# Last attention of a four-layer transformer on one core: reciprocal sums through device memory, and a row maximum in two parts

## The reference, cut to what matters

```
q = (LN(x) Wq) / 8                      # 1024 x 64
k = [LN(x) ; LN(ctx)] Wk                # 1101 rows: 1024 tokens and 77 of context
s = q k^T (+ mask on the 77)            # 1024 x 1101
p = exp(s - rowmax(s));  o = (p v) / rowsum(p)
x = x + gate * (LN(concat of heads o Wout) * g + b)
```

## Time and profile before

| | |
|---|---|
| Median of three runs | 2100.9 us |
| Profiled execution, its time | 2084.4 us |
| Profiled execution, its span | 2082.6 us |
| Busy: TensorE, VectorE, ScalarE, GpSimd | 1921.5, 1435.7, 978.5, 752.3 us |
| Mean granted TensorE clock over the span | 0.963 |
| Stage 6 | about 1096 to 1996 us of the span |

### The profile page before, as it was taken

How to read it: one execution, slowest core, us unless ns; L and a number is a source line. 1 busy time by engine, 2 the same in 40 slices (tenths; PEclk the granted TensorE clock), 3 DMA queues, 4 the chain that set the end, 5 groups by cost and what they waited for, 6 DMA issues and landing times.

```text
span 2082.6 us, 33216 instructions
## 1 busy us (share of the span) xinstructions
PE 1921.5 (92%) x11797; PEld 1355.2 (65%) x11797; DVE 1435.7 (69%) x2676; ACT 978.5 (47%) x2079; POOL 752.3 (36%) x1145
## 2 busy tenths in 40 slices
PE   6997799696999988997878999999999999998999
PEld 3885799542699976883565666666675666655644
DVE  5775111467344457787867999999878999998755
ACT  5672333343111252226875555555545555555455
POOL 1002111000522200000006777777656777777500
PEclk9897899898999999998989999999999999999999
DMA  3702899502489960002002333333222333333201
GB/s 115 208 2 79 273 323 333 170 1 86 163 292 321 310 228 1 1 1 86 1 13 60 82 83 82 83 83 83 72 57 72 82 82 82 82 82 81 63 1 41
DMA packets 191184, 226.87 MB, mean 109 GB/s; under 512 B 28939, under 2 KB 167085, under 8 KB 191021
## 3 DMA queue, kind: packets, MB, share of 16 engines
q1 hardware_dynamic: 183725, 201.98, 33.0%
q0 software_dynamic: 7296, 22.78, 3.3%
HBM read 127.64 MB, written 29.91 MB: 76 GB/s over the span
## 4 chain that ended last, share of the span: by engine, by line
PE 45%; ACT 6%; DVE 3%; issue 1%; POOL 0%; ACTq 0%; DVEq 0%; POOLq 0%
PE ps L640 41%; ACT w_odd L1796 4%; PE ps L1214 2%; PE ps L1215 1%; ACT arena L1785 1%; PE ps L1106 0%; DVE w_odd L2532 0%; DVE small L2410 0%; POOL arena L1908 0%; ACT out_feat L1708 0%; PE ps L1115 0%; ACT xn_tok L1651 0%; DVE small L2522 0%; ACT out_feat L1714 0%; DVE arena L2380 0%
## 5 line engine op out<-in xcount | busy, mean ns | idle before, releaser
L1908 POOL COPY arena<-w_odd 32x512 f32<-32x512 f32 x1024 | 623.7, 609 | 254.4 <-DVE w_odd L2532 202.1
L640 PE MATMUL ps<-arena,w_odd 128*128 128x128 f32 (+4 forms) x2352 | 468.2, 441 | 3.0 <-DVE arena L2202 1.2
L640 PE MATMUL ps<-arena 128*64 128x256 f32 (+4 forms) x3248 | 392.3, 370 | 8.3 <-DVE arena L2333 4.4
L640 PEld LDWEIGHTS ps<-arena 128*64 128x64 f32 (+4 forms) x3248 | 258.9, 155 | 119.5 <-issue 22.6
L2532 DVE STREAM_TRANSPOSE w_odd<-w_odd 128x1024 f32<-128x1024 f32 x256 | 317.4, 1245 | 14.6 <-ACT w_odd L1796 3.0
L1796 ACT ACTIVATE w_odd<-ps,small 128x1101 f32<-128x1101 f32 x256 | 301.6, 1179 | 48.0 <-DVE small L2522 41.0
L640 PEld LDWEIGHTS ps<-arena,w_odd 128*128 128x128 f32 (+3 forms) x2352 | 286.3, 188 | 27.9 <-issue 18.7
L1781 ACT ACTIVATE arena<-ps 77x256 f32<-77x256 f32 x128 | 48.5, 379 | 295.4 <-PE ps L1215 295.4
L2522 DVE TENSOR_REDUCE small<-ps 128x1 f32<-128x1101 f32 x128 | 166.9, 1304 | 29.3 <-PE ps L640 28.1
L1893 POOL DMA_INDIRECT token_rows<-arena x62 | 59.8, 964 | 292.3 <-DVE arena L2223 292.3
L2523 DVE TENSOR_REDUCE small<-ps 128x1 f32<-128x1024 f32 x128 | 155.4, 1214 | 0.0
(11 more groups left out here) (398 smaller groups left out, 2909.8 us busy)
## 6 DMA issues: line engine op xcount, KB each, us to landing
arena<-w_odd SPq DMA_DIRECT2D x1024, 64.0 KB
w_odd<-in_s_w SPq DMA_DIRECT2D x32, 1024.0 KB, 7.4
w_odd<-in_s_wgu SPq DMA_DIRECT2D x30, 704.0 KB, 6.1
w_even<-in_s_w SPq DMA_DIRECT2D x15, 1024.0 KB, 7.3
arena<-expert_rows_in SPq DMA_DIRECT2D x62, 130.0 KB, 4.7
w_odd<-in_s_wd SPq DMA_DIRECT2D x30, 256.0 KB, 3.6
out_feat<-in_s_wgu SPq DMA_DIRECT2D x10, 704.0 KB, 5.9
expert_rows_in<-zero_row POOLq DMA_DIRECT2D x1, 5070.0 KB, 33.2
```

Of the source, the lines that this page charges most:

```text
L640: return pe.matmul(o, lhsT, rhs, start=start, stop=stop, **kw)
L1908: pool.tensor_copy(s6_d[u % 4][32 * j:32 * j + 32, :, 256 * i:256 * i + 256], s6_pm[u % 2][32 * i:32 * i + 32, :, 256 * j:256 * j + 256]). ...
```

## The change

The diff has two parts. First, the reciprocals no longer become rows on TensorE. On even u, ScalarE issues a transfer of the four reciprocal columns of a group (128 partitions x 4 words) to a small array in device memory, written word by word; on the following odd u it waits for that transfer and issues two that read the rows back, each row broadcast over 64 partitions. `sums_turn`, its bank and ScalarE's copy L1785 go. VectorE's product waits for the transfers instead. Second, head 0's maximum is taken over bank 0 (512 columns) after the third count of a6_s, over the other 589 columns after the fourth, and the two are joined along two words.

```diff
+        rows_dram = nc.dram_tensor("sum_rows", [2, 2, 2, P], F32).ap()
...
-            if even and 2 <= u < NU + 2:
-                batch += [("r", (u - 2) // 2)]
...
-                def sums_turn(g):
-
-                    pe.wait_ge(a6_rb, g + 1)
-                    bank = free_bank(("r", g))
-                    for i in range(2):
-                        for h in range(2):
-                            r = 64 * h
-                            last = mm(PS[r:r + 64, bank, i * P:(i + 1) * P], s6_rc[:, g % 2, 2 * i + h:2 * i + h + 1].broadcast_to([P, DH]), ident[:, :])
-                    last.then_inc(r6_mm, 1)
...
-                    if even and 2 <= u < NU + 2:
-                        sums_turn((u - 2) // 2)
...
+                    if even and 2 <= u < NU + 2:
+                        g = (u - 2) // 2
+                        act.wait_ge(a6_rb, g + 1)
+                        if g >= 2:
+                            act.wait_ge(rows_in, 32 * (g - 1))
+                        act.dma_start(rows_dram[g % 2].rearrange("i h q -> q (i h)"), s6_rc[:, g % 2], allow_slow_non_contiguous=True).then_inc(rows_out, 16)
+                    if not even and 3 <= u < NU + 3:
+                        g = (u - 3) // 2
+                        act.wait_ge(rows_out, 16 * (g + 1))
+                        if g >= 2:
+                            copied(act, ("v", g - 2))
+                        for h in range(2):
+                            act.dma_start(s6_r[g % 2][64 * h:64 * h + 64].rearrange("p (i q) -> p i q", i=2),
+                                          rows_dram[g % 2][:, h].partition_broadcast(64)).then_inc(rows_in, 16)
...
-                    if even and 2 <= u < NU + 2:
-                        g = (u - 2) // 2
-                        bank = filled(("r", g))
-                        act.activation(s6_r[g % 2], PS[:, bank, 0:2 * P], ACT.Copy).then_inc(r6_act, 1)
...
-                        copied(dve, ("r", g))
+                        dve.wait_ge(rows_in, 32 * (g + 1))
                         dve.tensor_tensor(s6_ot[c][:, q0:q0 + 2 * P], PS[:, bank, 0:2 * P], s6_r[g % 2], ALU.mult).then_inc(r6_dve, 1)
...
+                        dve.tensor_reduce(s6_hm[:, u % 2, 0:1], psf[:, 0:512], AX.X, ALU.max, negate=True)
                         dve.wait_ge(a6_s, 4 * u + 4)
-                        dve.tensor_reduce(s6_nm[:, u % 2, 0:1], s6_sc[0], AX.X, ALU.max, negate=True).then_inc(a6_mx, 1)
+                        link(dve.tensor_reduce(s6_hm[:, u % 2, 1:2], psf[:, 512:KV], AX.X, ALU.max, negate=True))
+                        dve.tensor_reduce(s6_nm[:, u % 2, 0:1], s6_hm[:, u % 2], AX.X, ALU.min).then_inc(a6_mx, 1)
...
-                                dve.wait_ge(r6_mm, r6_no["r", g - 2] + 1)
+                                dve.wait_ge(rows_out, 16 * (g - 1))
```

More of the change, by code:

```diff
@@ L230, in build @@
         s6_gb = cut(small, 400, 4, KD)
-        s6_cm, s6_nm = cut(small, 420, 2, 2), cut(small, 424, 2, 2)
+        s6_cm, s6_nm, s6_hm = cut(small, 420, 2, 2), cut(small, 424, 2, 2), cut(small, 444, 2, 2)
         s6_sm, s6_rc = cut(small, 428, 2, 4), cut(small, 436, 2, 4)
@@ L307, in build @@
         r6_mm, r6_act, r6_dve = sem("r6_mm"), sem("r6_act"), sem("r6_dve")
+        rows_out, rows_in = sem("rows_out"), sem("rows_in")
         t6_done, copied6, t6_base = t5_c, t5_f, NT
@@ L394, in build @@
             for key in batch:
-                eng = "act" if key[0] in "crwn" else "dve"
+                eng = "act" if key[0] in "cwn" else "dve"
                 done[eng] += 1
```

## The result

The changed kernel takes 2221.18 us (median of four runs, 2217.63 to 2225.77), the kernel before 2101.62 beside it: ratio 1.0578, 95% interval 1.0561 to 1.0595, 119.6 us slower. The forecast was 2092.8.

What follows compares the result with a forecast made beforehand. TensorE bounds odd, projection and half the plain even stretches; the scores-maxima-exponentials loop bounds the other half. Terms -4.2, -1.4, -3.5, +1.0 total -8.1: 2084.4 to 2076.3, plus 16.5 to the median, 2092.8 us; range 2086 to 2108.

Steps and rivals of the forecast that it cites:

- Six projections: Six even stretches containing a projection, bound by TensorE alone: each 0.58 us shorter without the reciprocal products, -3.5 us.
- Even stretches: Even stretches without a projection: 26 from 6.35 and 27 from 6.24 to 6.19 us, -4.2 and -1.4.
- the extra work of VectorE: Split maximum gives VectorE 0.3 us more per unit; in odd units it sits before the exponentials, so not paid again.
- ScalarE's issues hidden: Three added transfer issues per group, 0.60 us each by SyncE's median, fall in ScalarE's idle time of 2.99 and 1.91 us.
- Rival C: Behind a projection ScalarE has no idle time; two issues cost 1.2 us each in six stretches: 2099.4 us, chance 0.14.
- The landings: Words and rows each have about 6 us to land; at two or three times 1.7 us, a microsecond or more spare.
- the 6 us that the prediction itself gave as a sign of being wrong: The forecast is wrong if words to device memory take over 6 us to land.
- The load: DMA engines: 512 one-word packets per group at 10 ns, up to 50 ns each (1.6 us per engine); delay taken as zero.
- Rival B: The words hold back SyncE's moves, so `weigh` waits in odd units; with a 2.0 us hold 2129 us, chance 0.14.
- Rival D: Longer TensorE waits lower the granted clock; in half of the odd stretches, some 1 us each: +30, 2123 us, chance 0.06.
- Rival A: Head 0's split maximum costs: overlap of short maxima fails, loop at 6.35 us, total 2101 us, chance 0.16.
- The end of the stage: After the last projection, the last rows arrive later than the last product wants them: +1.2 less about 0.2, +1.0 us.

Runs made afterwards that it cites:

- kernel 4: The changed kernel with reciprocals first transposed in 32 x 32 blocks on VectorE, so words leave as 128 packets of 128 bytes: 2110.49 us, ratio 1.0047.
- kernel 1: The kernel before with only head 0's maximum split in two parts, reciprocal rows still made on TensorE: 2097.88 us against 2101.73, ratio 0.9989.
- kernel 3: The kernel before, all its work kept, plus ScalarE's write of 512 single words per group to device memory, read by nobody: 2254.81 us, ratio 1.0722.
- kernels 7 to 9: The kernel before plus 512 one-word writes per group: into SBUF 64 bytes apart, 1.0002; device memory 512 bytes apart, 1.0009; device memory 64 bytes apart, 1.001.
- kernel 5: As kernel 4, but ScalarE issues the fetch of the rows only after both exponentials of the unit: 2106.03 us against 2100.08, ratio 1.002.
- kernel 7: The kernel before plus 512 one-word packets per group written into SBUF, 64 bytes apart, instead of device memory: 2100.17 us, ratio 1.0002.

## Why the prediction was wrong, step by step

**Six projections, -3.5.** Right: -4.0 in the kernel after. With the disturbance gone (kernel 4) -4.7.

**Even stretches, -5.6.** Right in mechanism and size. 6.16 or 6.17 against 6.19, and -5.1 in kernel 4. In the kernel after it is covered by four even stretches that grew by 19 us together (unit 32: 6.36 to 14.12, by stalled moves). Kernel 1 shows the split's own share, about 0.07 us in each of the 27. Wrong in one place: the extra work of VectorE, said to be not paid again in odd units, costs 0.25 us in each of the five odd stretches behind a projection (kernel 1), 1.2 us in all.

**ScalarE's issues hidden.** Right. The words' issue takes 0.37 us at the median, the rows' 0.63 (626 ns), where 0.60 was assumed for each. Rival C did not come: what the odd stretches behind a projection lost (5.99 to 6.24) they lose in kernel 1 too, which has no such issues.

**The landings, "a microsecond or more to spare".** Wrong for the words. I priced them as two or three times a move's 1.7 us, 3.4 to 5.1; they took 8.6 and 10.1 where the chain shows them, and over all 64 groups the landings are 7.5 to 10.4. That is beyond the 6 us that the prediction itself gave as a sign of being wrong. ScalarE's context copy stood behind that wait for 86 us in 19 cases. Kernel 3, where no one waits for them, is no faster, so this wait is not what made the loss; it is the same cause seen from the other side. Nearly right for the rows, 3.5 us at the median. Who waited for the transfers of this array in the kernel after (us, times), and the landing of the rows:

```profile
  ACT arena L1783: 86.0, 19
...
DMA to landing us min/median/max: 2.6/3.5/4.5
```

**The load, "up to 50 ns each ... so I take no delay".** This is the step that failed: a term put at nothing that measured 109.5 us, 83.5 of `weigh` waiting for moves that landed late and 26.0 of slower products behind these waits. The 10 ns came from packets that fill SBUF during the first loads, and in the trace of after the words' own records are even shorter, 7.4 ns. A record gives the engine's time for a packet; what the write holds up is in no record of its queue and appears as packets of q1 that last a microsecond. I bounded an unseen cost by rows of the wrong kind (other destination, other spacing), and the upper bound of 50 ns was a number with no row under it. Had I put it as landing time instead, the bound would have been open above.

**Rival B, 2129.** Its direction was right: `weigh` waits on odd units with the moves landing just before. Its mechanism was half right. It expected SyncE's issue to be held by the longest issue, 2.0 us. The count of issues over 0.8 us did not rise (40; before it was 41, not the 46 of the prediction), only the longest, from 1.99 to 4.04. So the making of descriptors is not shared with the words to any visible degree, and kernels 7 to 9 settle it: the same 512 packets from the same queue cost nothing. By the Trainium skill's "Perfetto Trace Analysis", DMA Instruction — HWDGE (DVE, Sync), the moves would queue in the making of descriptors; the issue rows do not bear it out. The Trainium skill's "DMA: Bandwidth & Descriptors", Rules for kernel authors, warned of one descriptor per element, and its advice would have avoided this; but the number of descriptors alone, 512, cost nothing measurable when they were 64 bytes or more apart (kernels 7 to 9). All 1024 issues of SyncE's moves in the kernel after; it answers to the earlier trace rows:

```profile
L629 SPq DMA_DIRECT2D arena<-w_odd x1024: 585/597/4042, 1120.0 to 2113.0; - x171
```

The price was wrong for two reasons: `weigh` waited up to 4.3 us where a hold of 2.0 was the ceiling, and the clock came on top. It had a chance of 0.14, and the stated range left its full price out.

**Rival D, the clock.** It was held apart as a rival and came as a consequence. In 14 units `weigh` waited 1.8 to 4.3 us and then took 5.4 to 7.1 us instead of 4.11; they hold 25 of the 26 us. In five others it waited 2.1 to 2.4 us and kept its 4.11. The plain waits for the exponentials, below a microsecond, which rival D had feared, cost no clock: 50 of the 58 even stretches stay at 6.16 or 6.17.

**Rival A.** Did not come: short maxima overlap.

**The end of the stage, +1.0.** +2.9 in the kernel after, +2.4 and +4.4 in kernels 4 and 5: mis-sized by 1 to 3 us, its parts not separated.

What stays open: why small writes that lie close together in device memory hold up the other queue, and from what closeness on. The runs show when it comes and what it costs, not where it arises. The changed kernel with the write repaired (kernels 4 and 5) has 12 to 15 us more in the odd stretches than before, which eat its gain of about 10: waits for moves and VectorE's added work, as taken apart above, and what delays the moves of kernel 5 is open.

## What to carry to other kernels

A transfer's own packets may look cheap while its writes hold up another queue: look at the neighbours' packets (a share over 100% for few bytes) and at the time to landing. Never scatter words side by side into a small stretch of device memory; either make the piece of one partition contiguous (16 bytes a piece was enough here: 0.2% instead of 7.2%) or space the words (64 bytes apart: 0.1%). And where a forecast's sign hangs on an operation that the trace does not show, measure it beside the work, read by nobody, before the kernel is rebuilt around it.

## What the runs showed of the hardware

- 512 one-word writes within 2 KB of device memory: 7.5 to 10.8 us to land (kernel after and kernel 3), and packets of another queue lasting over a microsecond in the meantime. 16 bytes apart: 2.6 us. 64 bytes apart: 1.9. 512 bytes apart: 1.8. The same bytes in 16-byte packets: 1.5.
- Packet records do not tell them apart: 7.6 ns each at the mean in kernels 3 and 8 alike.
- ScalarE issues a write of 2 or 16 KB to device memory in 0.33 to 0.37 us (medians), the 2 KB into SBUF of kernel 7 in 0.61, the 64 KB of broadcast rows in 0.63.
- Behind 3.11 us of idle TensorE a run of 36 products took 5.79 us instead of 4.11, at a granted clock of 0.60.
